# Layer 2 of a four-layer graph kernel: the probabilities turned by DMA in f16 parts instead of on TensorE in f32

## What is computed

```
h = maximum(layernorm(x), 0)
q, k, v = heads(h @ Wq.T + bq), heads(h @ Wk.T + bk), heads(h @ Wv.T + bv)
scores = einsum('bhqd,bhkd->bhqk', q, k) / sqrt(32)
scores = where(adj == 0, -inf, scores)
attn   = softmax(scores, axis=-1)
x = x + (einsum('bhqk,bhkd->bhqd', attn, v) as rows) @ Wo.T + bo
```

## Time and profile before

| what | value |
|---|---|
| median of three runs | 2096.86 us (2090.93 to 2097.89) |
| the profiled execution | 2089.51 us |
| its span, first to last instruction | 2087.9 us |
| mean granted clock of TensorE | 0.976 of full speed |
| TensorE busy with matmuls | 1905.1 us, 91% |
| VectorE busy | 1822.3 us, 87% |
| ScalarE busy | 1448.2 us, 69% |
| GpSimd busy | 609.8 us, 29% |
| DMA queues' packets | 6.1% of 16 engines' span |

### The profile page before, as it was taken

How to read it: one execution, slowest core, us unless ns; L and a number is a source line. 1 busy time by engine, 2 the same in 40 slices (tenths; PEclk the granted TensorE clock), 3 DMA queues, 4 the chain that set the end, 5 groups by cost and what they waited for, 6 DMA issues and landing times. The chain is left out here.

```text
span 2087.9 us, 45990 instructions
## 1 busy us (share of the span) xinstructions
PE 1905.1 (91%) x15944; PEld 1781.3 (85%) x15944; DVE 1822.3 (87%) x6095; ACT 1448.2 (69%) x3378; POOL 609.8 (29%) x756
## 2 busy tenths in 40 slices
PE   1899999999999999999999999999999999999985
PEld 1789888988888989888898888889888899898874
DVE  6688999989999988989998898999889899998774
ACT  2467677777677777767777776777776677876664
POOL 4122332222332332233233233323223322322222
PEclk8899999999999999999999999999999999999997
DMA  5000000000000000000000000000000000000000
GB/s 153 11 17 11 22 22 11 22 11 22 22 22 11 22 17 17 21 22 19 14 22 17 17 22 22 12 21 22 15 18 21 21 12 22 17 12 16 17 16 11
DMA packets 31206, 43.85 MB, mean 21 GB/s; under 512 B 3328, under 2 KB 26880, under 8 KB 30976
## 3 DMA queue, kind: packets, MB, share of 16 engines
q1 hardware_dynamic: 30976, 40.91, 6.1%
HBM read 32.38 MB, written 8.52 MB: 20 GB/s over the span
## 5 line engine op out<-in xcount | busy, mean ns | idle before, releaser
L707 POOL TENSOR_SCALAR ea<-ea,rs 128x256 f32<-128x256 f32 x256 | 140.0, 559 | 476.8 <-DVE rs L1316 476.8
L691 POOL TENSOR_TENSOR rstd<-ve,pow_half 128x2 f32<-128x2 f32 x160 | 119.4, 746 | 488.3 <-DVE ve L1197 486.2
L1093 PE MATMUL ps<-kp,qp 32*128 32x256 f32 x1536 | 250.1, 295 | 3.8 <-DVE kp L1345 3.4
L852 ACT ACTIVATE pb<-lg,hmin 128x256 f32<-128x256 f32 x512 | 231.6, 505 | 19.0 <-DVE hmin L1366 18.4
L899 PE MATMUL ps<-wout,hid 128*128 128x256 f32 x1536 | 230.2, 290 | 4.2 <-ACT hid L866 4.2
L1093 PEld LDWEIGHTS ps<-kp,qp 32*128 32x128 f32 x1536 | 197.7, 185 | 41.5 <-issue 22.9
L1366 DVE CUSTOM_DVE_ANT_0 lg<-ps,maskp 128x256 f32<-128x256 f32 x512 | 195.0, 417 | 33.8 <-PE ps L1093 31.2
L899 PE MATMUL ps<-pT,whs 128*128 128x256 f32 x1536 | 213.4, 288 | 11.0 <-DVE pT L1325 9.7
L899 PEld LDWEIGHTS ps<-pT,whs 128*128 128x128 f32 x1536 | 191.7, 191 | 20.5 <-DVE pT L1325 16.2
L899 PEld LDWEIGHTS ps<-wout,hid 128*128 128x128 f32 x1536 | 197.1, 190 | 6.4 <-ACT hid L866 5.6
L729 POOL TENSOR_TENSOR hid<-fu,hid 128x512 fp32r<-128x512 f32 x96 | 127.0, 1322 | 255.9 <-ACT hid L866 255.9
(11 more groups left out here) (180 smaller groups left out, 4739.6 us busy)
## 6 DMA issues: line engine op xcount, KB each, us to landing
tbc<-t_dram SPq DMA_DIRECT2D x32, 512.0 KB, 3.6
xin<-x_in SPq DMA_DIRECT2D x32, 256.0 KB, 2.7
out<-xs SPq DMA_DIRECT2D x32, 256.0 KB, 2.2
t_dram<-tb SPq DMA_DIRECT2D x128, 1.0 KB
xs<-a_heads SPq DMA_DIRECT2D x4, 128.0 KB, 5.9
pT<-a_heads SPq DMA_DIRECT2D x4, 128.0 KB, 4.6
lg<-W_out SPq DMA_DIRECT2D x2, 256.0 KB, 5.6
tb<-adj SPq DMA_DIRECT2D x1, 256.0 KB, 2.7
```

Source lines behind the costliest of these rows:

```text
L707: last = pool.tensor_scalar(ea(g)[:, c, :], ea(g)[:, c, :], rs[g][:, c:c + 1], 1.0, ALU.mult, ALU.mult)
L852: last = act.activation(pb[h % 2][:, c, :], lg[h % 2][:, c, :], ACT.Exp, bias=hmin[h % 2][:, c:c + 1], scale=-1.0)
L1093: last = pe.matmul(bank(BA)[:, c, :], qp[r, a, oc, blk(c)], kp[r, b, oc, :], start=(n == 0), stop=(n == 2))
```

## The change

- The two parts are made before the turn. `p16_hi` (ScalarE) copies the exponential from `lg` to `p16[:, 0]` in f16, and `p16_lo` (GpSimd) writes the difference to `p16[:, 1]`. Both read and write SBUF. The exponential is written over `lg`; `pb` is gone, `p16` has two buffers, `lg` and `hmin` have three.
- `p_T` is one DMA with `transpose=True`, issued by SP: 128 partitions x 1024 f16 values (256 KB), turned in 8 blocks of 128x128 to `pT16`. It waits for `p16_lo` and, from the third head on, for the `values` of two heads before. `values` waits for its landing, and so does the `p16_hi` of two heads later.
- `scores` go to bank BA and BB in turn, so they wait for the minimum of two heads before.
- The planner's costs follow: `p_T` 2.0 on SP, and the way from TensorE, VectorE and GpSimd to SP is 0.2 instead of 5.0. This changes the order of all engines.
- The weights that are staged at the start pass through one buffer less (13 instead of 14).

```diff
@@
-        lg = [sb(f"lg{k}", [P, C, N]) for k in range(2)]
-        pb = [sb(f"pb{k}", [P, C, N]) for k in range(2)]
+        lg = [sb(f"lg{k}", [P, C, N]) for k in range(LG)]
+        p16 = [sb(f"p16{k}", [P, 2, C, N], F16) for k in range(2)]
@@
-        HOP = ((0.0, 0.2, 0.2, 0.2, 5.0), (0.22, 0.15, 0.15, 0.17, 0.2), (0.25, 0.13, 0.13, 0.16, 5.0),
-               (0.16, 0.07, 0.06, 0.1, 5.0), (3.5, 3.5, 3.5, 3.5, 0.0))
+        HOP = ((0.0, 0.2, 0.2, 0.2, 0.2), (0.22, 0.15, 0.15, 0.17, 0.2), (0.25, 0.13, 0.13, 0.16, 0.2),
+               (0.16, 0.07, 0.06, 0.1, 0.2), (3.5, 3.5, 3.5, 3.5, 0.0))
@@
-                a("scores", h, TE, 0.7, ("q_lo", 0), ("k_lo", 0), ("smin", h - 1))
-                a("smin", h, VE, 0.69, ("scores", h), ("s_exp", h - 2))
-                a("s_exp", h, SC, 0.8, ("smin", h), ("p_T", h - 2))
-                a("p_T", h, TE, 0.44, ("s_exp", h), ("pT16_lo", h - 1))
-                a("pT16_hi", h, SC, 0.5, ("p_T", h), ("values", h - 2))
-                a("pT16_lo", h, VE, 0.6, ("pT16_hi", h))
-                a("values", h, TE, 0.37, ("pT16_lo", h), ("v_c", 0), ("gather", h // 2 - 1) if h % 2 == 0 else ("values", h - 1))
+                a("scores", h, TE, 0.7, ("q_lo", 0), ("k_lo", 0), ("smin", h - 2))
+                a("smin", h, VE, 0.69, ("scores", h), ("p16_lo", h - LG))
+                a("s_exp", h, SC, 0.8, ("smin", h))
+                a("p16_hi", h, SC, 0.52, ("s_exp", h), ("p_T", h - 2))
+                a("p16_lo", h, PO, 1.2, ("p16_hi", h))
+                a("p_T", h, SY, 2.0, ("p16_lo", h), ("values", h - 2))
+                a("values", h, TE, 0.37, ("p_T", h), ("v_c", 0), ("gather", h // 2 - 1) if h % 2 == 0 else ("values", h - 1))
@@
+                def transpose_probs(h, u):
+                    sp.wait_ge(p16_lo, of(u, h, HQ))
+                    if h >= 2:
+                        sp.wait_ge(o_done, of(u, h - 2, HQ))
+                    sp.dma_start(pT16[h % 2][:].rearrange("p t c n -> p (t c n)").rearrange("p (m n) -> p m n", n=P),
+                                 p16[h % 2][:].rearrange("p t c n -> p (t c n)"), transpose=True)\
+                        .then_inc(p_turned[h % 2], 16)
@@
+                def low_of_probs(h, u):
+                    pool.wait_ge(p16_hi, of(u, h, HQ))
+                    pool.tensor_tensor(p16[h % 2][:, 1], lg[h % LG][:], p16[h % 2][:, 0], ALU.subtract).then_inc(p16_lo, 1)
@@
                 def softmax_exp(h, u):
                     act.wait_ge(min_ready, of(u, h, HQ))
+                    for c in range(C):
+                        last = act.activation(lg[h % LG][:, c, :], lg[h % LG][:, c, :], ACT.Exp,
+                                              bias=hmin[h % LG][:, c:c + 1], scale=-1.0)
+                    last.then_inc(p_done, 1)
+
+                def high_of_probs(h, u):
+                    act.wait_ge(p_done, of(u, h, HQ))
                     if h >= 2:
-                        act.wait_ge(p_turned, of(u, h - 2, HQ))
...
-                    act.activation(pT16[h % 2][:, 0], bank(BB), ACT.Copy).then_inc(pT16_hi, 1)
+                        act.wait_ge(p_turned[h % 2], 16 * of(u, h // 2 - 1, HQ // 2))
+                    act.activation(p16[h % 2][:, 0], lg[h % LG][:], ACT.Copy).then_inc(p16_hi, 1)
@@
-                    else:
-                        pe.wait_ge(min_ready, of(u, h - 1, HQ))
+                    elif h >= 2:
+                        pe.wait_ge(min_ready, of(u, h - 2, HQ))
...
-                def transpose_probs(h, u):
-                    pe.wait_ge(p_done, of(u, h, HQ))
-                    if h:
-                        pe.wait_ge(pT16_lo, of(u, h - 1, HQ))
-                    transpose_to(BB, pb[h % 2]).then_inc(p_turned, 1)
-
                 def values(h, u):
-                    pe.wait_ge(pT16_lo, of(u, h, HQ))
+                    pe.wait_ge(p_turned[h % 2], 16 * of(u, h // 2, HQ // 2))
@@
                 def score_minimum(h, u):
                     dve.wait_ge(s_done, of(u, h, HQ))
-                    if h >= 2:
-                        dve.wait_ge(p_done, of(u, h - 2, HQ))
+                    if h >= LG:
+                        dve.wait_ge(p16_lo, of(u, h - LG, HQ))
...
-                def low_of_turned(h, u):
-                    dve.wait_ge(pT16_hi, of(u, h, HQ))
-                    dve.tensor_tensor(pT16[h % 2][:, 1], bank(BB), pT16[h % 2][:, 0], ALU.subtract)\
-                        .then_inc(pT16_lo, 1)
```

More of the change, by code:

```diff
@@ L121, in adj_preln_kernel @@
         dmin, zz, npeak, psums, rs = (columns_of(n, HG + 2) for n in ("dmin", "zz", "npeak", "psums", "rs"))
-        hmin = [sb(f"hmin{k}", [P, C]) for k in range(2)]
+        hmin = [sb(f"hmin{k}", [P, C]) for k in range(LG)]
         rden = sb("rden", [P, 2 * C])
@@ L173, in adj_preln_kernel @@
         loaded = [sem(f"loaded{k}") for k in range(XI)]
-        lent = [t[:] for t in (lg[0], lg[1], pb[0], pb[1], cx, rb, fu, ea3[0], ea3[1], tb3[0], tb3[1], tb1, ea1, xs[0])]
+        lent = [t[:] for t in (lg[0], lg[1], lg[2], cx, rb, fu, ea3[0], ea3[1], tb3[0], tb3[1], tb1, ea1, xs[0])]
         adj_i, adjt_i, adj_f, adjt_f, linked = lent[-5:]
@@ L573, in adj_preln_kernel @@
                     ("q", "k", "v", "q_hi", "q_lo", "k_hi", "k_lo", "v_a", "v_r", "v_b", "v_c", "scores", "smin",
-                     "s_exp", "p_T", "pT16_hi", "pT16_lo", "values", "gather", "normal", "x_bo", "wo", "x3"),
+                     "s_exp", "p_T", "p16_hi", "p16_lo", "values", "gather", "normal", "x_bo", "wo", "x3"),
                     (), ("out_b2", "ffn1", "f1_full", "f1_hi", "f1_lo", "ffn2", "y", "y_gamma", "final", "store"))
@@ L643, in adj_preln_kernel @@
         v_a, v_r, v_b, v_c = (sem(n) for n in ("v_a", "v_r", "v_b", "v_c"))
-        s_done, min_ready, p_done, p_turned = (sem(n) for n in ("s_done", "min_ready", "p_done", "p_turned"))
-        pT16_hi, pT16_lo, o_done, o_used = (sem(n) for n in ("pT16_hi", "pT16_lo", "o_done", "o_used"))
+        s_done, min_ready, p_done = (sem(n) for n in ("s_done", "min_ready", "p_done"))
+        p16_hi, p16_lo, o_done, o_used = (sem(n) for n in ("p16_hi", "p16_lo", "o_done", "o_used"))
+        p_turned = each("p_turned", 2)
         wo_done = sem("wo_done")
@@ L677, in spread @@
                     sp.dma_start(tbc[:], t_dram[u % 2:u % 2 + 1].broadcast_to([P, HG, N])).then_inc(t_spread, 16)
-                program = dict(load=load, store=store, t_spread=spread)
+                def transpose_probs(h, u):
[5 more added lines that the diff above has]
+                        .then_inc(p_turned[h % 2], 16)
+                program = dict(load=load, store=store, t_spread=spread, p_T=transpose_probs)
                 for name, k, u in order:
@@ L880, in _ @@
                                q_hi=high_of_q, k_hi=high_of_k, v_a=value_first, v_b=value_second,
-                               s_exp=softmax_exp, pT16_hi=high_of_turned, hid_hi=high_of_hidden,
+                               s_exp=softmax_exp, p16_hi=high_of_probs, hid_hi=high_of_hidden,
                                f1_full=whole_ffn, f1_hi=high_of_ffn)
@@ L935, in transpose_rows @@
                     elif t == TR_CTX:
-                        pe.wait_ge(pT16_lo, of(u, HQ - 1, HQ))
+                        pe.wait_ge(min_ready, of(u, HQ - 1, HQ))
                     elif u:
@@ L1111, in values @@
                         for n, (part, kc) in enumerate(((0, 0), (0, 1), (1, 0), (1, 1))):
-                            last = pe.matmul(ps[:, at0:at0 + VC], pT16[h % 2][:, part, kc, blk(c)],
+                            last = pe.matmul(ps[:, at0:at0 + VC], pT16[h % 2][:, part, c, blk(kc)],
                                              v3[:, kc, h, :], start=(n == 0), stop=(n == 2 * C - 1))
@@ L1141, in _ @@
                                st_rows=score_rows, s_cols=source_columns, probs_T=transpose_attention, k=key, v=value, scores=scores,
-                               p_T=transpose_probs, values=values)
+                               values=values)
                 of_some = {("spread", GOUT): spread_output_targets, ("wh", 0): second_weights}
```

22 lines of the change are left out of this document (8 added, 14 removed).

## The result

The changed kernel takes 2323.09 us in the median of four runs (2322.04 to 2328.45), the kernel before 2093.89 us beside it. The ratio is 1.110 (95% interval 1.107 to 1.113): 229 us slower. The forecast was 2042 us, faster, within 1950 to 2230.

What follows compares the result with a forecast made beforehand. TensorE's own work was taken as the bound. The sum was 2088 - 118 - 12 + 90 + 15 - 30 = 2033 us, and 9 us more for the runs' median gave 2042 us, range 1950 to 2230.

Steps and rivals of the forecast that it cites:

- The bound: TensorE's own work sets the pace, busy 95% from 400 to 1900 us; VectorE close behind at 91%.
- the new ones: TensorE's waits at `values` for the turn's landing, read at three pairs a batch over 32 batches: 90 us added.
- L: Time from the last part to the turn's landing: taken as 4.0 us, bounds 2.2 to 5.9; said to decide the sign.
- this rival: The DMA turn done in 8 blocks, one after another: L 9.1 us, kernel 2429 us in the median; chance 0.11.
- The turns leave TensorE, 118 + 12 us: 256 turns leave TensorE, saving 0.46 us each, 118 us, and their waits on VectorE, 12 us.
- GpSimd: 256 new subtractions, 338 us on GpSimd, hold VectorE's SBUF-only operations: 56 us more there, 15 us (0 to 56) on the path.
- What comes back, 30 us: A third of TensorE's 94 us of idle time merges with new waits or goes because VectorE is freer.
- The clock: TensorE's granted clock, 0.99 from 400 to 1900 us, to be looked at if TensorE loses more than its waits.
- The rivals: Four cases for the DMA turn: quick 0.13, gain and waits cancel 0.10, turn as bound 0.21, blocks in a row 0.11.
- The slower one: The DMA turn replaces the work as the bound, L of 5 to 7 us: 2165 us at 6, up to 2242; chance 0.21.

Runs made afterwards that it cites:

- LEAD 40, 20: Changed kernel, planner given 1.25 us on SP and 1.9 to landing per turn, layer weights 40, 20, 5, 10 instead of 30, 10, 5, 10: 2063.75 us.
- order for the measured turn: Changed kernel, same steps, planner given 1.25 us on SP and 1.9 to landing per turn instead of 2.0 and 3.5: 2114.45 us, ratio 1.009 to before.
- the spare work: Kernel before in its own order, plus 256 subtractions of 128x512 on GpSimd whose result nothing uses: 2147.53 us, ratio 1.025.
- the short low part: Changed kernel, GpSimd's low part made of 8 columns per chunk instead of 256: 2275.62 us in its order, 2052.79 us planned with the measured turn.

## Why the prediction was wrong, step by step

- *The bound.* Right for the kernel before: TensorE's own work set the pace. The step that failed is the next one, that TensorE's other waits would be those of before less a third, while the new ones would lie at `values`. I read the new list only at three pairs of `values` a batch, and took the rest of it for as well filled as the old one. At `values` TensorE waited 5.4 us in 1500, where I had put 90 over the span (some 50 at the measured turn); its whole idle time was 216 us instead of 73.5, nearly all of it elsewhere. The diff named the cause: the planner's numbers were changed, and all five lists with them. "It does another order" was no rival of its own, and the runs give it 209 of 229 us. That 7 of a batch's 8 scores stood ahead of its first `values` was no sign of it: with LEAD 40, 20, the fastest order with all the steps, it is 6 or 7 as well. What I didn't look at is how far layer 2 runs ahead of layer 3.
- *L.* Taken 4.0, measured 3.1, inside 2.2 to 5.9. I wrote that the sign would hang on L alone. It hung on the L that the planner believed: 5.5 us. The bounds from the plain DMAs were good; the Trainium skill's 1309 ns for 128x128 (VectorE: DVE Perf Modes, The three transpose paths) times eight would have been 10.5 us as an estimate, and no turn took more than 5.8. So the trace rejects this rival, with 10.5 us and with its own 9.1 (its eight DMAs of 1.15 us make 9.2).
- *The turns leave TensorE, 118 + 12 us.* Not seen by itself. Without GpSimd's new work and in an order for the measured turn the gain over before is 41 us, so some 90 of the 130 us don't arrive there. By the two pages TensorE's busy time falls by 101 us, where 118 of its time were forecast, and its idle time over the span rises by 63 us (183 to 246), where 12 were to go. So most of what is missing is waits, among them 16 us in the stretch of `values` for a landing; the clock is 0.952 over the span instead of 0.976.
- *GpSimd.* 1180 ns a subtraction, not 1322, 301 us instead of 338. VectorE's busy time: forecast 1704, measured 1712; with the spare work in the kernel before 62.5 us more, forecast 56. The size on VectorE was right for the kernel before. The mechanism was read too widely: operations "that live in SBUF alone" don't all stand still, the statistics of the norms and the reciprocals never do. The share on the path was too small: I took a quarter, 15 us (0 to 56), and it was 52 us of VectorE's 62.5 with the spare work; the short low part gave 47 us back beside 56 of VectorE's, and 62 beside 95 in the order for the measured turn, both with the shorter chain in them. A likely reason, argued only: among VectorE's stopped operations are the small ones (peak, norms) that others wait for.
- *What comes back, 30 us.* Nothing came back: TensorE's idle time over the span rose from 183 to 382 us, and even without the low part, in the order for the measured turn, to 246.
- *The clock.* Named as a thing to look at, without a price. In the stretch it went from 0.99 to 0.89; the turns left 157 us, and the matmuls' busy time still rose by 33. Of the 208 us between the changed kernel and the one planned with the measured turn, about half (100 us) is the same matmuls taking longer, and the prediction had no term for it.
- *The rivals.* All four were about L or about blocks. The slower one decided from L = 5 on; at the measured L my own sum gives some 2000 us. The result lies above the range for a reason that no case had in it.

## What to carry to other kernels

Where the order of work is made by a planner, a change of its costs is a change of everything, and has to be priced as a part by itself: plan the old steps with the new numbers, and look at the whole list for the work that now stands alone. Give such a planner measured lengths before judging a change by its time; a length that is too long raises the rank of all that stands before it, once for every time the longest path goes through the step, and the damage can come all at once (0.75 us more of SP's time in the plan: 199 us). A GpSimd operation on two SBUF operands cost the VectorE beside it between a fifth and two fifths of its length, depending on the order (62.5 us for 297 us of GpSimd in the kernel before, 95 for 242 in the order for the measured turn), and most of that was seen in the kernel's time (52 and 62 us).

## What the runs showed of the hardware that was not expected

A DMA that turns 128x1024 f16 values within SBUF lands in 3.1 us (3.0 at least, 5.8 at most, 256 times), 1.23 us of which SP is held; the 256 turns brought 270,336 packets under 512 B, 1056 each, and beside them the load and the spread took 2.8 and 3.7 us, 2.7 and 3.6 before. TensorE's granted clock was 0.883 over a span of which it was busy 84%, with a window of 20 us at 0.57 that held waits of 3.3 and 3.1 us, and 12 matmuls then took 2.93 instead of 1.59 us. Beside GpSimd's subtractions, VectorE's TENSOR_SCALAR and its operations with two SBUF inputs were held for up to 1.1 us (168 to 1125 ns, 218 to 1341), while BATCH_NORM_STATS2, BATCH_NORM_AGGREGATE and RECIPROCAL on SBUF never were (430, 183 and 168 ns at most).
